# Fixed PSUM banks for two projections, an earlier weight split and token shifts on one engine, in a recurrent feed-forward block

## The reference

```python
x1 = x + og * g @ Wo.T
xc = _ln(x1, ln2_w, ln2_b)
sx2 = jnp.concatenate([state[:, 0:1] - xc[:, :1], xc[:, :-1] - xc[:, 1:]], axis=1)
xk2 = xc + sx2 * ffn_maa_k
xr2 = xc + sx2 * ffn_maa_r
rr = jax.nn.sigmoid(xr2 @ Wfr.T)
kk = jnp.square(jax.nn.relu(xk2 @ Wfk.T))
return x1 + rr * (kk @ Wfv.T)
```

## Time and profile before

| | before |
|---|---|
| median of 3 runs | 4241.41 us (4233.95 to 4247.2) |
| the profiled execution | 4250.26 us, span 4248.5 us |
| TensorE busy, matmul | 3740.6 us, 88% |
| VectorE busy | 2618.1 us, 62% |
| ScalarE busy | 2156.9 us, 51% |
| GpSimd busy | 1669.7 us, 39% |
| granted TensorE clock, mean | 0.948 of full |

### The profile page before, as it was taken

How to read it: one execution, slowest core, us unless ns; L and a number is a source line. 1 busy time by engine, 2 the same in 40 slices (tenths; PEclk the granted TensorE clock), 3 DMA queues, 4 the chain that set the end, 5 groups by cost and what they waited for, 6 DMA issues and landing times. The chain is left out here.

```text
span 4248.5 us, 66434 instructions
## 1 busy us (share of the span) xinstructions
PE 3740.6 (88%) x24448; PEld 2278.7 (54%) x24448; DVE 2618.1 (62%) x5675; ACT 2156.9 (51%) x4272; POOL 1669.7 (39%) x1865
## 2 busy tenths in 40 slices
PE   7988899898888989989888998998988889899898
PEld 4544565545545456555554545655555454565555
DVE  5765646666576564566657656456665765646665
ACT  5655733434666573343366657334336675733433
POOL 4554542232454454223245444422324544542222
PEclk9999999899999999999989999999999999999899
DMA  4032211102204222010220322101022032220102
GB/s 135 15 107 64 81 69 41 59 21 100 75 15 122 55 83 71 32 59 31 90 76 26 108 65 75 69 31 59 31 90 77 27 108 65 75 69 31 59 32 98
DMA packets 94558, 276.11 MB, mean 65 GB/s; under 512 B 25472, under 2 KB 25984, under 8 KB 73088
## 3 DMA queue, kind: packets, MB, share of 16 engines
q1 hardware_dynamic: 94208, 271.58, 19.8%
HBM read 201.24 MB, written 4.19 MB: 48 GB/s over the span
## 5 line engine op out<-in xcount | busy, mean ns | idle before, releaser
L805 POOL TENSOR_SCALAR probs<-probs,row_inv 128x512 f32<-128x512 f32 x1024 | 693.1, 693 | 643.9 <-DVE row_inv L720 643.9
L664 ACT ACTIVATE probs<-probs,row_max 128x512 f32<-128x512 f32 x1024 | 733.1, 725 | 130.8 <-DVE row_max L736 129.6
L559 PE MATMUL ps<-ident,probs 128*128 128x128 f32 x4096 | 609.8, 291 | 170.6 <-ACT pT L658 144.3
L559 PEld LDWEIGHTS ps<-ident,probs 128*128 128x128 f32 x4096 | 481.2, 147 | 381.1 <-ACT pT L658 206.9
L658 ACT ACTIVATE pT<-ps 128x512 f32<-128x512 f32 x768 | 429.8, 602 | 113.2 <-PE ps L559 112.7
L369 PE MATMUL ps<-mix,wring 128*128 128x512 f32 x1024 | 471.0, 596 | 3.5 <-DMA wring<-in_blocks_dram 3.4
L534 PE MATMUL ps<-kstack,qstack 96*128 96x512 f32 (+1 forms) x1024 | 383.4, 469 | 16.7 <-DMA qstack<-hi 7.1
L736 DVE CUSTOM_DVE_ANT_0 probs<-ps,maskA 128x512 f32<-128x512 f32 x512 | 329.3, 681 | 43.9 <-PE ps L534 43.9
L736 DVE CUSTOM_DVE_ANT_0 probs<-ps,neg 128x512 f32<-128x512 f32 x512 | 340.5, 685 | 8.9
L369 PEld LDWEIGHTS ps<-mix,wring 128*128 128x128 f32 x1024 | 191.2, 190 | 198.7 <-issue 179.3
L1532 POOL TENSOR_TENSOR hinv<-hvar,minus_half 128x32 f32<-128x32 f32 x24 | 146.2, 6092 | 377.3 <-DVE hvar L1254 377.3
(11 more groups left out here) (177 smaller groups left out, 7056.4 us busy)
## 6 DMA issues: line engine op xcount, KB each, us to landing
wring<-in_blocks_dram SPq DMA_DIRECT2D x151, 1024.0 KB, 5.0
qstack<-hi SPq DMA_DIRECT2D x256, 64.0 KB, 2.0
kstack<-hi SPq DMA_DIRECT2D x256, 64.0 KB, 2.0
maskA<-in_mask_dram SPq DMA_DIRECT2D x9, 1024.0 KB, 7.4
rows<-in_rows_dram SPq DMA_DIRECT2D x8, 1024.0 KB, 4.6
qstack<-hi SPq DMA_DIRECT2D x256, 32.0 KB, 2.0
qstack<-lo SPq DMA_DIRECT2D x128, 64.0 KB, 2.0
kstack<-lo SPq DMA_DIRECT2D x128, 64.0 KB, 2.0
```

What stands on the lines that cost most here:

```text
L559: ins = nc.tensor.transpose(tile[:, qc * P:(qc + 1) * P], probs[:, m % PSLOTS, qc, kc * P:(kc + 1) * P], ident[:, :])
L664: nc.scalar.activation(p, p, ACT.Exp, bias=row_max[:, n % PSLOTS, qc:qc + 1], scale=-1.0, accum_out=row_sum[:, n % PSLOTS, qc:qc + 1]).the ...
L805: nc.gpsimd.tensor_scalar(p, p, row_inv[:, (n - 1) % PSLOTS, qc:qc + 1], 1.0, ALU.mult, ALU.mult)\
```

## The change

Four edits in the recurrent layers.

1. The four `fr` tiles go to banks 4, 5, 6 and 7 and the four `fv` tiles to banks 0 to 3, by name and not by `take`. At the end of the stage TensorE waits for the last sigmoid.
2. The high part of the `fk` weights is made on ScalarE before `y_out` of the last head group, where it was made after the square root; the low part on VectorE stands before `low_part('gated', 2, 2)`, where it stood after `low_part('gated', 3, 2)`.
3. In the feed-forward, all four shifts are made by VectorE; GpSimd makes none. (In the first half of the layer GpSimd keeps chunks 1 and 3.)
4. On ScalarE the high part of `xk2` chunk c follows the norm of chunk c+2, where all four norms came first.

```diff
-        def act_norm(act, tag, out, wcol, bcol, shift=0, parts=False):
-            for c in range(C):
+        def act_norm(act, tag, out, wcol, bcol, shift=0, parts=False, chunks=range(C)):
+            for c in chunks:
...
             for tc in range(C):
-                to_N3(pe, take(pe, 'fr', l, tc), f'fr_{l}', (act_hi[:, 1], act_lo[:, 2]), tc, tile_ready.reach('fr', l, tc),
+                to_N3(pe, ps[:, RING0 + tc, :], f'fr_{l}', (act_hi[:, 1], act_lo[:, 2]), tc, tile_ready.reach('fr', l, tc),
                       ready=(lambda fc: pe.wait_ge(*dve_done.when('xr2_lo', l, fc))) if tc == 0 else None)
             parts_wait(pe, f'fv_{l}')
             for tc in range(C):
-                to_N3(pe, take(pe, 'fv', l, tc), f'fv_{l}', (act_hi[:, 2], act_lo[:, 3]), tc, tile_ready.reach('fv', l, tc),
+                to_N3(pe, ps[:, tc, :], f'fv_{l}', (act_hi[:, 2], act_lo[:, 3]), tc, tile_ready.reach('fv', l, tc),
                       ready=(lambda fc: pe.wait_ge(*dve_done.when('kk_lo', l, fc))) if tc == 0 else None)
+            pe.wait_ge(*act_emptied.when('fr', l, C - 1))
...
                 def shift(c):
                     dve.wait_ge(*act_emptied.when('lnT', tag, c))
-                    if c % 2:
+                    if c % 2 and tag[0] == 'a':
                         dve.wait_ge(*pool_done.when('sx', tag, c))
                         return
...
                                 shift(c)
-                                if c % 2 == 0:
+                                if c % 2 == 0 or tag[0] == 'f':
                                     dve.wait_ge(*dve_done.when('sx', tag, c))
...
             low_part('gated', 1, 2)
+            dve_w(dve, f'fk_{l}')
             low_part('gated', 2, 2)
             variance_out(C - 1)
             inverse_root(C - 1)
             normalise(C - 1)
             gated(C - 1)
             low_part('gated', C - 1, 2)
-            dve_w(dve, f'fk_{l}')
...
-                nc.vector.tensor_tensor(recT[:, tc, :], ps[:, ring.bank('fv', l, tc), :], gT[:, tc, :], ALU.mult)\
+                nc.vector.tensor_tensor(recT[:, tc, :], ps[:, tc, :], gT[:, tc, :], ALU.mult)\
...
             high_part('gated', 1, 2, dve_done.when('gated', l, 1))
+            act_w(act, f'fk_{l}', dve_done.when('r8', l, C - 1), tile_ready.when('kt', l, C - 1))
             y_out(C - 1)
             high_part('gated', 2, 2, dve_done.when('gated', l, 2))
             act.wait_ge(*dve_emptied.when('var', l, C - 1))
             nc.scalar.activation(hroot[:, :, :], hvar[:, :, :], ACT.Sqrt).then_inc(*act_done.reach('root', l, C - 1))
-            act_w(act, f'fk_{l}', dve_done.when('r8', l, C - 1), tile_ready.when('kt', l, C - 1))
             high_part('gated', C - 1, 2, dve_done.when('gated', l, C - 1))
-            act_norm(act, f'f{l}', xa, f'ln2_w_{l}', f'ln2_b_{l}', shift=1)
-            for c in range(C):
-                high_part('xk2', c, 1, dve_done.when('xk2', l, c))
+            for c in range(C + 2):
+                if c < C:
+                    act_norm(act, f'f{l}', xa, f'ln2_w_{l}', f'ln2_b_{l}', shift=1, chunks=(c,))
+                if c >= 2:
+                    high_part('xk2', c - 2, 1, dve_done.when('xk2', l, c - 2))
...
-                nc.scalar.activation(gT[:, tc, :], ps[:, ring.bank('fr', l, tc), :], ACT.Sigmoid)\
+                nc.scalar.activation(gT[:, tc, :], ps[:, RING0 + tc, :], ACT.Sigmoid)\
...
-                for c in (1, 3):
+                for c in (1, 3) if tag[0] == 'a' else ():
                     pool.wait_ge(*act_emptied.when('lnT', tag, c))
                     nc.gpsimd.tensor_tensor(sx[:, c, :], xa[:, c, 0:L], xa[:, c, 1:L + 1], ALU.subtract)\
```

## The result

The changed kernel takes 4187.31 us (median of 4 runs, 4173.83 to 4194.35), where the kernel before takes 4242.26 (median of 4). The ratio is 0.9874, with a 95% interval of 0.9852 to 0.9896. A second measurement, with five runs, gave 4183.49 and 0.9864 (0.9843 to 0.9885). The forecast was 4187.5. The kernel is thus 1.3% faster, and the interval excludes no change.

The account below looks back on a forecast made before the run. TensorE, busy 88%, was taken to lose time in three pauses and at its lower clock. Terms 5.15 + 1.19 + 0.4 = 6.74 us a stage, times 8 = 54; 4241.4 - 54 = 4187.5 us, range 4173 to 4208.

Parts of the forecast that it names:

- The sum: Recurrent layers' feed-forward stage: 5.15 + 1.19 + 0.4 = 6.74 us gained a stage, 54 us over eight stages.
- Edit 1: Receptance and value products: no pause before the fourth receptance tile; 5.15 us a stage, some 3.3 pause and restart, 1.7 clock.
- the bounds: Limits on edit 1's gain: 3.3 us if the slow stretch comes anyway, 5.2 if all goes.
- Edits 3 and 4: Before the key product: second mix 0.35 us earlier, first low part 0.84 shorter; 1.19 us a stage, edit 4 securing 0.25.
- The cover to watch: Receptance mix before its product: slack falls to 0.3 us; the stage loses 0.15 if GpSimd's split doesn't move.
- Edit 2: Before the addition of `wo`: key-weight split moved ahead, root 0.55 to 0.65 us later, yet 0.4 us gained a stage.
- under 2 was the sign: Sign in the profile after: addition of `wo` starts less than 2 us after `wo` chunk 3 starts.
- The clock that doesn't come back: Rival: the slow stretch is elsewhere in the stage; 5.0 us gained a stage, 4201 us; 9%.
- the split that costs: Rival: the split moved ahead lies whole in the root's chain; 4.8 us gained a stage, 4203 us; 10%.
- the tile that isn't freed: Rival: something else ends the fourth receptance tile's wait at the same time; 1.6 us gained a stage, 4229 us; 3%.
- the slower case: Rival: granted clock falls within products running 33 us without a pause; stage loses net 7.7 us, 4303 us; 3%.
- The one for more: Rival: the next stage also starts sooner at a better clock; 8 us in all, 4179 us; 5%.

Follow-up runs that it names:

- the filled pause: Changed kernel with the wait for the first sigmoid put back before the fourth receptance tile, and 13 further products filling that pause; 4206.7 us, one run.
- the bare wait: Changed kernel with TensorE again waiting for the first sigmoid before the fourth receptance tile, banks still fixed, pause not filled; 4232.84 us, one run.
- The two experiments that delay the key product by 0.30 and 0.37 us: Changed kernel with all four norms before the high parts (4193.43 us); changed kernel with chunk 1's feed-forward shift on GpSimd again (4195.46 us).
- The kernel with the low part on VectorE: Changed kernel with key-weight split further ahead, first-half shifts on VectorE, and the receptance weights' low part on VectorE instead of GpSimd; 4171.54 us.
- the kernel before it: Changed kernel with the key weights' high part ahead of the third gate on ScalarE and first-half shifts also on VectorE; 4177.63 us.
- the fill of the norm: 27 unread TensorE products a stage in the norm's pauses, added to the kernel with the receptance weights' low part on VectorE; 4139.21 us.

## Why the prediction was right, point by point

**The sum.** 6.74 us a stage were forecast and 6.66 measured. The total then came out within 1 us of the forecast, which is luck: runs of one kernel differ by up to 26 us. The sum also left out the share outside the stages, 3688 to 3723 us over the fourteen profiles, which goes largely with the number of the recurrence's stops (3.4 us a stop, an estimate by a straight line through the fourteen).

**Edit 1**, forecast 5.15: measured 4.98 in seven stages. The term was short by one detail: the last matmul counts with its full 0.39 us, not with the spacing of 0.2266. That the squares' low parts and the mixers' split are covered was right to the digit for the latter, 0.71 us of slack in layer 2 where 0.7 was forecast. Its split of the gain into 3.3 us of pause and 1.7 of clock stands as well: the filled pause gave 3.7 and 1.6 for a wait that was 0.3 us longer. What the bounds did not hold is a stage like the two of the bare wait in which the clock costs twice as much; none occurred in the kernel before.

**Edits 3 and 4**, forecast 1.19: measured 1.21 at the start of the key product, in its two terms 0.37 and 0.84, with 0.30 lost if the norms come first (0.25 forecast). What the prediction did not say is how much of it arrives. The two experiments that delay the key product by 0.30 and 0.37 us leave the stage as long as it was. In slow stages a key product that starts sooner takes the longer: 12.9 to 13.1 us in six of the eight stages after, and 12.6 to 12.9 in the slow stages of those two experiments. In fast ones the receptance mix is next.

**The cover to watch** was named rightly, the receptance mix behind GpSimd's split, with 0.3 us of slack and 0.15 to lose. The size was wrong where the key product runs fast. It took 11.18 us in one stage after, and then the receptance product waited 0.23 and 0.30 and ran its first tile in 4.0 us instead of 2.7, as its input came. The value column is 15.19 instead of 13.87, 1.3 us given back. The kernel with the low part on VectorE shows that cause by taking it away: 13.87 in its three fast stages, where the one fast stage of the kernel before it still had 15.20.

**Edit 2**, forecast 0.4: measured 0.53. The addition of `wo` now starts 1.00 us after `wo` chunk 3 (under 2 was the sign), where it was 2.06. The root came 0.63 us later, as forecast, but the transposes behind it only 0.48, for TensorE had been a little late for them before.

**The rivals.** The clock that doesn't come back, the split that costs, the tile that isn't freed and the slower case each have a run against them: full clock with edit 1 alone, 0.53 gained with edit 2 alone, no wait in the value column, 13.8 us at clock 1.00. The rival on the falling clock fails for the long stream itself: after the key product's slow start the clock is 1.00 from 795.5 to the end of the value product, and in all eight stages it is 1.00 over the receptance and value products. The one for more, that a stage starts at a better clock, had 5% and happened in one stage of eight, but 1.3 of the some 1.9 us that it returned there were eaten by the receptance mix.

## What to carry to other kernels

A ring of PSUM banks ties a product to the engine that reads the bank, in the order of that engine's list; where the reader has a long piece of other work first, a bank by name for one more tile saves the wait and the half clock behind it. When work is moved to an idle engine, look for a whole gap: in the list of ScalarE the same split cost the root 0.6 us in one place and nothing a few instructions earlier. Where TensorE's pause can't be avoided, products that nobody reads keep the clock up, here 1.9 us a stage, and intervals between named events, stage by stage, show what the total hides: differences of 0.3 us stood there in every profile, while ten runs of the kernel without edit 1 did not show in the total the 11.8 us by which its eight stages are shorter.

## What the runs showed of the hardware

**The clock before the key product.** In all 104 stages of the thirteen profiles without the fill of the norm, the granted clock falls to half during the norm, where TensorE makes transposes between waits for VectorE. What differs is what happens then. In the kernels with a pause of 3.1 us before the key product (before, edit 1 alone, edit 2 alone), half clock lasted on into the product in 15 of 24 stages; in the other nine it had ended before the product and came again 0.1 to 1.0 us behind its start. With the pause at 1.9 to 2.3 us (ten profiles) it lasted on in 41 of 80 stages and came again, 0.9 to 1.5 us behind the start, in 12. In the other 27 it had ended 1.2 to 1.8 us before the product and did not come again: these are the fast stages. With the pauses of the norm filled the clock never fell, in 8 of 8. Three windows of the changed kernel: the first 6 us of the key product in a slow stage, then the norm and the first 6 us of the key product in the fast stage (granted clock 0.62, 0.50 and 1.00):

```profile
789.50:795.50 6.00, 5.96 (x17) 4.76 (x18) 5.82 (x9) 3.32 (x4) 0.11 (x1) 0.62 0.00 0
...
1828.30:1835.00 6.70, 3.97 (x15) 2.98 (x15) 4.47 (x9) 2.83 (x5) 1.62 (x4) 0.50 0.00 0
1836.40:1842.40 6.00, 5.95 (x26) 4.99 (x27) 5.83 (x9) 3.31 (x4) 0.10 (x1) 1.00 0.00 0
```

Which stages are fast differs from profile to profile, so that like stages of one kernel differ by up to 1.3 us in the changed kernel and 2.8 with the low part on VectorE. So a shorter pause has a second, uncertain return, which no sum of durations from one profile shows; work in the pause makes it certain.

**Stops without a releaser.** TensorE stopped 6 to 16 times in a program, at fixed places of its list, all within runs of 128 small products. The stops lasted 1.4 to 2.2 us, save seven shorter ones (0.2 to 1.2 us). Of the 168 over 0.9 us, 143 had a stretch at half clock behind them. At about 3.6 us each (an estimate from the pieces above) the stops are worth 22 to 58 us, up to as much as the whole change, and they differ between two executions of one kernel: 14 and 11 in the two profiles of the changed one.
